# Second attention: a head pair's scores as one rounded-fp32 product over 96 stacked rows, the halves relaid through DRAM

## The reference, cut to what matters

```python
qh = (q @ Wq + bq).reshape(B, LQ, HEADS, D_K).transpose(0, 2, 1, 3)
kh = (k @ Wk + bk).reshape(B, LKV, HEADS, D_K).transpose(0, 2, 1, 3)
...
scores = jnp.einsum('bhqd,bhkd->bhqk', qh, kh) * scale
attn = jax.nn.softmax(scores, axis=-1)
out = jnp.einsum('bhqk,bhkd->bhqd', attn, vh)
...
return concat @ Wo + bo
```

## Time and profile before

| what | value |
|---|---|
| median of 3 runs | 510.99 us (510.92 to 511.07) |
| profiled execution, first to last instruction | 509.3 us (its own total is not listed) |
| TensorE busy | 479.0 us, 94% |
| VectorE busy | 383.8 us, 75% |
| ScalarE busy | 258.0 us, 51% |
| GpSimd busy | 147.5 us, 29% |
| mean granted TensorE clock | 0.987 |

### The profile page before, as it was taken

One profiled execution on the slowest core, in us unless ns is written; L12 is line 12 of the kernel. 1 busy time (PEld: TensorE's weight loads), 2 busy tenths in 40 slices (PEclk: granted clock), 3 DMA queues, 4 the chain that ended last, 5 costly groups with the idle time before them and its releaser, 6 DMA issues.

```text
span 509.3 us, 8629 instructions
## 1 busy us (share of the span) xinstructions
PE 479.0 (94%) x3258; PEld 407.4 (80%) x3258; DVE 383.8 (75%) x771; ACT 258.0 (51%) x396; POOL 147.5 (29%) x123
## 2 busy tenths in 40 slices
PE   6999999999999999999999759999999999999991
PEld 4777789898887777777777528988999998999991
DVE  4799999899998867979778896557667575748441
ACT  2667788776865654555546314344434443444120
POOL 4364100010001202212013127115072827354253
PEclk9999999999999999999999979999999999999997
DMA  6523000000000001210311543035364737372041
GB/s 209 157 83 73 24 2 1 0 1 1 1 2 0 24 19 42 84 54 31 125 42 42 167 134 98 18 72 143 105 137 145 154 105 164 94 168 47 1 42 20
DMA packets 37166, 36.06 MB, mean 71 GB/s; under 512 B 6458, under 2 KB 35974, under 8 KB 36998
## 3 DMA queue, kind: packets, MB, share of 16 engines
q1 hardware_dynamic: 30665, 27.65, 17.6%
q0 software_dynamic: 6144, 7.66, 9.1%
q10 hardware_dynamic: 317, 0.21, 0.1%
HBM read 27.70 MB, written 8.39 MB: 71 GB/s over the span
## 4 chain that ended last, share of the span: by engine, by line
PE 65%; DVE 23%; issue 6%; ACT 3%; DMA 2%; POOL 1%; DVEq 0%; ACTq 0%; POOLq 0%
PE PS L1477 14%; PE PS L1478 14%; PE PS L1479 14%; PE PS L1893 5%; PE PS L1837 4%; PE PS L1750 3%; DVE tmp L1139 3%; DVE tmp L1128 3%; DVE hT_lo L1147 3%; PE PS L1497 3%; PE PS L1902 3%; DVE tmp L1116 1%; DVE xn L995 1%; DVE nmaxC L1170 1%; DVE tmp L1119 1%
## 5 line engine op out<-in xcount | busy, mean ns | idle before, releaser
L1477 PE MATMUL PS<-w_hi,hT_hi 128*128 128x256 f32 x384 | 110.3, 287 | 0.1
L1479 PE MATMUL PS<-w_hi,hT_lo 128*128 128x256 f32 x384 | 108.6, 283 | 0.0
L1478 PE MATMUL PS<-w_lo,hT_hi 128*128 128x256 f32 x384 | 108.6, 283 | 0.0
L939 ACT ACTIVATE tmp<-PS,biasT 128x512 f32<-128x512 f32 (+1 forms) x80 | 43.8, 600 | 111.0 <-PE PS L1479 111.0
L664 POOL DMA_INDIRECT out<-tmp,dst_idx x32 | 55.8, 1744 | 99.5 <-DVE tmp L1433 92.8
L1477 PE MATMUL PS<-xT_hi,w_hi 128*128 128x512 f32 (+1 forms) x224 | 81.1, 362 | 0.4 <-DVE xT_lo L1003 0.4
L1478 PE MATMUL PS<-xT_lo,w_hi 128*128 128x512 f32 (+1 forms) x224 | 80.7, 360 | 0.0
L1479 PE MATMUL PS<-xT_hi,w_lo 128*128 128x512 f32 (+1 forms) x224 | 80.5, 359 | 0.0
L1477 PEld LDWEIGHTS PS<-w_hi,hT_hi 128*128 128x128 f32 x384 | 73.4, 191 | 3.3 <-issue 2.3
L1478 PEld LDWEIGHTS PS<-w_lo,hT_hi 128*128 128x128 f32 x384 | 73.5, 191 | 0.8
L1479 PEld LDWEIGHTS PS<-w_hi,hT_lo 128*128 128x128 f32 x384 | 73.5, 191 | 0.0
(11 more groups left out here) (261 smaller groups left out, 865.8 us busy)
## 6 DMA issues: line engine op xcount, KB each, us to landing
w_raw<-in_L_ffn_w SPq DMA_DIRECT2D x72, 256.0 KB, 3.3
residual<-in_x SPq DMA_DIRECT2D x4, 512.0 KB, 5.5
out<-residual SPq DMA_DIRECT2D x3, 512.0 KB, 4.5
normed_rows<-xn SPq DMA_DIRECT2D x3, 512.0 KB, 2.9
kv<-in_L_ffn_b SPq DMA_DIRECT2D x1, 1024.0 KB, 6.6
tmp<-in_L_xattn_Wq SPq DMA_DIRECT2D x2, 256.0 KB, 5.6
out<-residual SPq DMA_DIRECT2D x2, 256.0 KB, 5.1
normed_rows<-xn SPq DMA_DIRECT2D x2, 256.0 KB, 4.0
```

What stands on the lines that cost most here:

```text
L939: act.activation(gD[:, G % 2, f, 0:P * n], H[:, G % 2, f, 0:P * n], ACT.Gelu, bias=biasT[:, col:col + 1]).then_inc(e_gelu, 1)
L1477: pe.matmul(o, lh, rh, start=start, stop=False, skip_group_check=skip)
L1478: pe.matmul(o, lh, rl, start=False, stop=False, skip_group_check=skip)
L1479: return pe.matmul(o, ll, rh, start=False, stop=stop, skip_group_check=skip)
```

## The change

The query and key are split into a rounded half and a rest. A pair's scores become one product over 96 rows with rounded-fp32 operands: the query's rows hold half, rest, half and the key's rows half, half, rest, or the like, so the product is half times half plus the two mixed terms. The stacked layout puts parts of different rows of the queries on 96 partitions, so each part is written to scratch in DRAM (`query_parts`, `key_parts`) and read back into its place, all on the SP queue.

- `scores`: 8 products a tile, each 96 rows by 154 columns, no longer in separate strips; the waits between its sets are gone.
- `copy_queries` writes the rounded half (`q_high`), and VectorE's new `query_rest` the rest (`q_low`), 2 instructions of 512 columns per chunk.
- `stack_queries(c)` on SP: 4 writes of 256 KB, then 3 reads of 256 KB for the chunk's first two tiles and 3 for its last two (9 and 9 smaller ones for chunk 0). `scores_ready` makes TensorE wait for them.
- `split_keys` (ScalarE) and one subtraction (GpSimd) at the start of the feed-forward part; `stack_keys` reads them back.
- Everything of chunk c + 1 moves one step ahead: `apply` to step 4c, transposes, `x_hi` and `x_lo` to 4c + 1, the queries to 4c + 2. For chunk 0 `queries_of(0)` moves ahead of `project(11)`, `logits_columns(0)` ahead of step 1.
- `split_gate` and the row statistics of chunk 1 move ahead of `shift(0)`.
- The splitting of the experts' weights moves to later steps, the last two on GpSimd behind the last scores.

```diff
-HIGH_AT = [1, 3, 5, 7, 9, 11, 13, 14]
+COLUMNS_AT = {4: 1, 8: 2, 12: 3}
+HIGH_AT = [4, 5, 8, 9, 10, 11, 13, 14]
...
+            def stack_queries(c):
+
+                sp.wait_ge(qhigh_ready, KD * (c + 1))
+                for h in range(2):
+                    here = slice(256 * h, 256 * h + 256)
+                    sp.dma_start(query_parts[c, 0].rearrange("p (m n) -> p m n", m=KD)[:, :, here],
+                                 q_high[c][:, :, here].bitcast(F32)).then_inc(qhigh_saved, 16)
+                sp.wait_ge(q_copied, KD * (c + 1))
...
+                for h in range(2):
+                    here = slice(256 * h, 256 * h + 256)
+                    for q, part in ((0, 0), (2, 0), (1, 1)):
+                        if h == 0 and q == 0:
+                            sp.wait_ge(qhigh_saved, 32 * (c + 1))
+                        if h == 0 and q == 1:
+                            sp.wait_ge(qlow_saved, 32 * (c + 1))
+                        rows = query_parts[c, part].rearrange("(s r) (m n) -> r m s n", s=4, m=KD)
...
+            def query_rest(c):
+
+                if c == 3:
+                    dve.wait_ge(qlow_saved, 32 * c)
+                for m in range(KD):
+                    dve.wait_ge(qhigh_ready, KD * c + m + 1)
+                    dve.scalar_tensor_tensor(out=q_low[c][:, m, :], in0=T[:, m, :],
...
             def scores(t, i):
...
-                if i >= 1:
-                    pe.wait_ge(c_scores, 3 * t + i)
                 for pair in score_set(i):
...
-                for o, rows, m in places:
-                    ins = pe.matmul(o, qT[rows, m, here], Kpar[rows, m, b, :, :], start=True, stop=True)
+                    ins = pe.matmul(SC[:, bank, 2 * KEYS * slot:2 * KEYS * slot + 2 * KEYS],
+                                    home[0:96, pair - first, here], KS[b][0:96, pair, :], start=True, stop=True)
                 ins.then_inc(c_scores, 1)
+            def scores_ready(t):
+
+                c, h = t // 4, t % 4 // 2
+                if t % 2 == 0:
+                    pe.wait_ge(q_stacked[h], 16 * (9 + 3 * c))
+                if t % (NT // 2) == 0:
+                    pe.wait_ge(k_stacked[2 * t // NT], 48)
```

More of the change, by code:

```diff
@@ L247, in flamingo_gated_two_layers, with flat @@
         minus_ident = w_hi[:, 6, 1, 0, 0:P]
+        def flat(t):
+            return t.rearrange("p a b c d -> p (a b c d)")
+        KS = [flat(w_hi[:, 6:8, :, :, :])[:, 768:768 + 16 * KEYS].rearrange("p (u n) -> p u n", n=2 * KEYS),
+              flat(w_lo[:, 2:4, :, :, :])[:, 0:16 * KEYS].rearrange("p (u n) -> p u n", n=2 * KEYS)]
+        QS_first = [(0, 6, flat(w_lo[:, 4:7, :, :, :]).rearrange("p (u n) -> p u n", n=512)),
+                    (6, 8, flat(w_hi[:, 4:5, :, :, :]).rearrange("p (u n) -> p u n", n=512))]
+        QS_odd, QS_even = [h[:, :, :, :].rearrange("p a b n -> p (a b) n") for h in (hT_hi, hT_lo)]
+        QS = [QS_first, [(0, 8, QS_odd)], [(0, 8, QS_even)], [(0, 8, QS_odd)]]
+        q_high = [hT_lo[:, 0, :, :] if c == 1 else xT_hi[:, 1, :, :] for c in range(NC)]
+        q_low = [hT_lo[:, 1, :, :] if c == 1 else xT_lo[:, 1, :, :] for c in range(NC)]
         bias_hl, bias_hi = w_hi[:, 6, 0, 0, 0:P], w_hi[:, 6, 0, 1, 0:P]
@@ L342, in flamingo_gated_two_layers @@
         q_ready = sem("q_ready")
+        qhigh_ready = sem("qhigh_ready")
         q_copied = sem("q_copied")
+        qhigh_saved = sem("qhigh_saved")
+        qlow_saved = sem("qlow_saved")
+        q_stacked = [sem(f"q_stacked{h}") for h in range(2)]
+        khigh_ready = sem("khigh_ready")
+        klow_ready = sem("klow_ready")
+        k_saved = sem("k_saved")
+        k_stacked = [sem(f"k_stacked{b}") for b in range(2)]
         c_scores = sem("c_scores")
@@ L529, in _, with stack_keys @@
                 place_values(j, h)
-            for u in range(PAIRS, 2 * PAIRS + 1):
-                load_unit(u)
+            def stack_keys(b):
+                for q, part in enumerate((0, 1, 0)):
+                    src = key_parts[(0, 0, 1)[q]].rearrange("(s r) (m b n) -> r b m s n", s=4, m=KD, b=2)[:, b, :, :, :]
+                    sp.dma_start(KS[b][32 * q:32 * q + 32, :, :].bitcast(F32).rearrange("r (m s) n -> r m s n", m=KD),
+                                 src).then_inc(k_stacked[b], 16)
@@ L1183, in _ @@
                         ffn_residual(g // PAIRS - 1)
+                    if g == NB_PAIRS - 1:
+                        query_rest(0)
                     if g == 0:
@@ L1261, in _ @@
                 c = t // 4
+                if t == 1:
+                    rows_logits(0)
                 if 1 <= t < NT:
@@ L1266, in _ @@
                 if t < NT:
+                    if t % 4 == 0 and c + 1 < NC:
+                        apply(round_of(2, c + 1))
                     if t % 4 == 1 and c + 1 < NC:
-                        apply(round_of(2, c + 1))
+                        x_lo(round_of(2, c + 1))
                     if t % 4 == 2 and c + 1 < NC:
-                        x_lo(round_of(2, c + 1))
+                        query_rest(c + 1)
                     if t in APPLY_AT:
@@ L1774, in _ @@
                     hidden(g)
+                    if g == NB_PAIRS - 1:
+                        pe.wait_ge(late_split, 1)
+                        queries_of(0)
                     if g == 0:
@@ L1812, in logits_columns @@
                 logit_chunks[0] += 1
+            logits_columns(0)
             def logits_rows(c):
@@ L1863, in _ @@
                     scores(t, 1)
+                if t == 1:
+                    logits_rows(0)
                 if 1 <= t <= NT:
```

129 lines of the change are left out of this document (93 added, 36 removed).

## The result

The changed kernel takes 513.57 us, the median of 16 runs (511.1 to 518.74); the kernel before, beside it, 511.03 (510.75 to 511.5). The ratio is 1.0052, 95% interval 1.0033 to 1.0071: 0.5% slower. The forecast was 508.8, 0.4% faster. 513.57 is inside the range given, on the wrong side of no change; the rival "the relay is late" is what happened. The spread is new too: 7.6 us where the kernel before has 0.8.

A forecast was written before the change was run, and what follows sets the result against it. TensorE was taken to set the attention's pace, VectorE close behind. Feed-forward's end 5.9, step 1 -1.8 + 1.2, scores -12.0 and VectorE stalls 4.5 sum to -2.2 us: 508.8, forecast's own range 507 to 510, overall 506.8 to 514.2.

The forecast's parts named there:

- the relay is late: Rival: queries' write and read through DRAM take longer, TensorE waits in three chunks; 514.3 us with 3 us more; chance 0.24.
- The relay, costed at nothing: Chunks 1 to 3: stacked queries land at 13.2 to 13.5 us, TensorE wants them at 15.2; some 1.5 us spare.
- its point of decision: Relay rival: it decides the outcome from about 0.7 us of lateness a chunk.
- Its branch on the ports: Relay rival: reads into 32 partitions at half rate, 1.6 to 2.4 us in all, 511 to 513 us; chance 0.1 of 0.24.
- The product: Scores on TensorE: eight products and ten transposes save 0.8 us a tile, 12.0 us over tiles 1 to 15.
- the floor of 0.118: Scores on TensorE: each new product takes 0.118 us, set by loading 128 weights; eight make 0.94.
- The feed-forward's end: Ahead of the attention: queries 2.9, rests 1.3 and statistics 2.2 us, 0.5 absorbed in gaps; shift(0) 5.9 us late.
- VectorE's share: Attention: VectorE's loop stalls TensorE 1.5 us each behind steps 3, 7 and 11, 4.5 us in all.
- 12.0 + 1.8 - 1.2 - 4.5: Attention: 12.0 us from scores, 1.8 from logits_columns(0) moved, less 1.2 for step 1's softmax loop and 4.5 of VectorE stalls.
- three of the four named: Sign: TensorE should wait for the exponential in steps 8, 9, 12 and 13.
- the forecast 90%: Sign: VectorE should be busy over 90% of steps 4 to 7.
- GpSimd's last subtractions, costed at nothing: Splitting of experts' weights: GpSimd's last two subtractions end long before the experts, so no cost.

The follow-up runs named there:

- e2_free_scores: Changed kernel, but chunks 1 to 3 scored from chunk 0's stacked queries, their own writes and reads still sent with nobody waiting; 509.63 us, ratio 0.9966.
- e7_end: Kernel with the sooner relay, plus chunk 0's queries behind project(11) again and ScalarE's copies behind the gelus of pair 15; 516.66 us, ratio 1.0103.

## Why the prediction was wrong, by its own steps

**The relay, costed at nothing, is the step that failed.** It claimed 1.5 us to spare. In chunk 1 of the changed kernel, counted like the prediction from the first transpose of step 2 (177.34): queries 5.0 (5.0 forecast), ScalarE's copies 6.2 (6.3), rests 7.3 (7.0). Then it parts.

The writes had landed at 11.0, not 10.1: SP needs 0.6 us to issue each, which the sum left out, and the rests were 0.3 later. The third read took 5.4, not 3.1: the median of the earlier trace rows was that of wide reads, with fewer transfers around them. Of the excess of 2.3, the run with reads held back takes off 1.1 and the run with wide reads 0.5; the last 0.7 was not told apart. So the stack was there at 16.4. (In chunks 2 and 3 the third read took 5.8 and 6.0.) And TensorE was ready at 14.5, not 15.2, since the steps are 0.2 to 0.3 shorter than I had them. That is 1.9 us late in place of 1.5 early.

In the next two chunks TensorE waited 2.2 and 2.4 us, and at the second halves not at all. The waits sum to 6.3 us, half clock behind scores(8) on top; the medians say 4.0 (without relay) and 3.9 (sooner relay), as part of it covers VectorE's own lag. So it was the write and read times taken at their medians, the issue time left out, and a consumer taken too late, that made a term of nothing out of 4 us.

The rival had the mechanism and, with 3 us in all, 514.3; it deserved more than 0.24: 2.2 us lay between the forecast and its point of decision, and the issue time (0.6), the steps that the change itself shortens (0.7) and the narrow reads that it names (0.6) use up 1.9 of them. Its branch on the ports, 1.6 to 2.4 us in all, fits the third reads of chunks 2 and 3 (1.9 less when wide) but not that of chunk 1 (0.5 less).

**The product.** 0.8 to 1.0 a tile against 0.8, 12 to 14.7 us over 15 tiles in place of 12.0. Right in sum, not in its parts: the floor of 0.118 was 0.13, and the ten transposes took 0.9 us, not 1.16. Why they are cheaper between the new products, no run shows.

**The feed-forward's end.** 5.9 forecast, 7.1 measured. By rows: queries 2.8 (2.9), rests 1.3 (1.3), statistics 2.0 (2.2). Missing was 1.0 for GpSimd's subtraction of the keys, a stretched VectorE instruction at 52 us; and the 0.5 that should have fallen into VectorE's gaps did not. The 2.0 of the statistics is no loss by itself: with the relay of chunk 0 covered, putting them back cost 4.2, as they are due ahead of shift(1) anyway.

**VectorE's share.** The windows from tile 0's to tile 15's maxima, the kernel before and then the one with the sooner relay:

```profile
159.75:277.61 117.86, 115.83 (x869) 89.87 (x868) 95.81 (x261) 63.57 (x110) 23.95 (x19) 1.00 0.16 50
```

```profile
166.92:274.49 107.57, 101.75 (x736) 88.33 (x735) 96.38 (x257) 62.08 (x109) 21.42 (x17) 1.00 0.45 132
```

The stretch is 10.3 us shorter, where the forecast had 12.0 + 1.8 - 1.2 - 4.5 = 8.1. TensorE's busy time fell by 14.1, close to the 13.8 forecast; its idle time rose by 3.8, from 2.0 to 5.8, where the forecast had 5.7. Of the 5.8, 1.4 are still waits for the relay; in `e2_free_scores`, with no such wait, the waits for VectorE and ScalarE in the same stretch are 5.8, 4.0 more than before. So the two held TensorE back, and by less than I took. (A part of each wait hides in the modelled ends of the records, so the true figures are somewhat higher.) In the trace without relay 3.4 us of such waits lie between 190 and 262 us, all in steps 8, 9 and 12, three of the four named. VectorE's 29.04 of 32.30 us just misses the forecast 90%.

**GpSimd's last subtractions, costed at nothing.** They did end long before the experts, but one ran beside VectorE's last normalising and made it 2 us longer, of which 1.0 reached the end.

**The sum with the relay covered**, from the trace of the sooner relay, is +7.2 to tile 0's maxima, -10.3 to tile 15's and +1.5 to the end: -1.6, where the forecast had +5.9, -8.1 and nothing, -2.2. That the two are so near is luck: errors of +1.3, -2.2 and +1.5 nearly cancel. The runs measure -1.8 with the sooner relay and -1.7 without one.

## What to carry to other kernels

A relay through DRAM is costed as a chain with a clock beside it: issue time of every transfer on its queue, landing under the load that the relay itself makes, shape of the destination, and the moment the consumer will want it after the change, not before it. What is wanted first is written and read first, and the rest held back; that alone turned 0.5% slower into 0.3% faster. And before a step is moved on an engine that runs in order, list what it then stands behind and what stands behind it: the same move of the queries gave +6.9 us with its copies in the wrong place and -2.7 with the scores behind a project.

## What the runs showed that I had not expected

- A VectorE instruction on SBUF operands that starts while a GpSimd one runs ends only after it: 1.23 to 2.33, 1.22 to 2.41, 0.74 to 2.76 for two, 1.38 to 2.80 for four. One that started first is not stretched, and GpSimd's then is.
- The late relay widened the spread of the runs, its traffic did not: 7.6 us with it, 1.2 with the same transfers and no wait, 0.8 before. The wait alone doesn't explain it, as `e7_end` waits 9.3 us for a DMA and its 6 runs spread over 1.4. The granted clock goes with it: the five runs of the changed kernel below 512.1 us have a mean of 0.980 to 0.987, the three above 516 one of 0.967 to 0.971. In the trace the lower clock came behind one of three waits of about 2 us; that this is what varies from run to run is likely, and not shown.
